# A state-space mixer with a top-1 mixture of experts: when the rows of the closing sum are fetched, and where the last expert units run

## The reference, cut to what matters

```
xn = layernorm(x)                                   # per token
proj = xn @ in_proj_w.T                             # gate 512 | x 512, B 128, C 128 | dt 64
xBC = silu(conv_b + causal 4-tap conv(xBC))
dt = softplus(dt + dt_bias);  A = -exp(A_log)       # 64 heads of 8
y = ssd(x * dt, dt * A, B, C) + D * x               # state recurrence along the sequence
hg = y * silu(gate)
s = (hg * rsqrt(mean(hg * hg) + 1e-5) * norm_w) @ out_proj_w.T

route = sigmoid(xn @ router_w)                      # 8 experts, each token goes to its best one
f = (silu(xn @ gate_w[e]) * (xn @ up_w[e])) @ down_w[e] * route[e]

out = x + s * silu(f)
```

## Time and profile before

| | |
|---|---|
| median of 3 runs | 488.84 us |
| the profiled execution | 490.0 us, its span 488.2 us |
| TensorE busy with matmuls | 417.5 us (86%), 2506 matmuls |
| TensorE loading weights | 340.5 us (70%) |
| VectorE | 310.7 us (64%), 675 instructions |
| ScalarE | 197.9 us (41%) |
| GpSimd | 215.8 us (44%) |
| moved by DMA | 81.43 MB, mean 167 GB/s |

### The profile page before, as it was taken

One profiled execution on the slowest core, in us unless ns is written; L12 is line 12 of the kernel. 1 busy time (PEld: TensorE's weight loads), 2 busy tenths in 40 slices (PEclk: granted clock), 3 DMA queues, 4 the chain that ended last, 5 costly groups with the idle time before them and its releaser, 6 DMA issues. The chain is left out here.

```text
span 488.2 us, 7643 instructions
## 1 busy us (share of the span) xinstructions
PE 417.5 (86%) x2506; PEld 340.5 (70%) x2506; DVE 310.7 (64%) x675; ACT 197.9 (41%) x490; POOL 215.8 (44%) x252
## 2 busy tenths in 40 slices
PE   0779376609999999999999999999989999998862
PEld 0775123409888797988788899788678878987752
DVE  4504975244598483769598664649687666667578
ACT  1552359310642626342633635442633662262100
POOL 3200471373018271718236455508236447776840
PEclk9999669757999999999999999999999999999785
DMA  8940126622464555776575563856575624313695
GB/s 274 287 118 1 49 104 230 203 83 88 142 178 167 178 182 180 186 225 186 186 209 194 155 211 118 222 187 173 178 213 186 159 99 127 108 57 100 193 349 188
DMA packets 56055, 81.43 MB, mean 167 GB/s; under 512 B 4720, under 2 KB 34416, under 8 KB 55888
## 3 DMA queue, kind: packets, MB, share of 16 engines
q1 hardware_dynamic: 54144, 75.81, 50.8%
q0 software_dynamic: 1872, 5.13, 2.9%
HBM read 64.37 MB, written 16.56 MB: 166 GB/s over the span
## 5 line engine op out<-in xcount | busy, mean ns | idle before, releaser
L577 POOL TENSOR_TENSOR ARENA<-ARENA 128x512 f32<-128x512 f32 (+1 forms) x80 | 105.1, 1323 | 7.8 <-ACT ARENA L782 2.8
L1009 PEld LDWEIGHTS BANK<-ARENA 128*128 128x128 f32 x736 | 87.6, 197 | 22.7 <-ACT ARENA L818 16.1
L1009 PE MATMUL BANK<-ARENA 128*128 128x128 f32 x736 | 89.1, 280 | 16.5 <-ACT ARENA L818 15.9
L629 POOL DMA_INDIRECT gate_rows<-ARENA x23 | 23.0, 998 | 155.8 <-DVE ARENA L1307 67.5
L899 PE MATMUL BANK<-ARENA,W_MAIN 128*128 128x512 f32 x160 | 80.5, 655 | 11.4 <-DVE ARENA L1206 11.4
L1187 DVE SCALAR_TENSOR_TENSOR ARENA<-BANK,CONVC,ARENA 128x511 f32<-128x511 f32 (+2 forms) x72 | 53.6, 748 | 28.1 <-ACT ARENA L725 15.9
L1042 DVE TENSOR_TENSOR ARENA<-ARENA,BANK 128x256 f32<-128x256 f32 (+1 forms) x128 | 57.5, 449 | 17.0 <-POOL ARENA L643 11.9
L899 PEld LDWEIGHTS BANK<-ARENA,W_MAIN 128*128 128x128 f32 x160 | 32.6, 213 | 49.4 <-issue 33.9
L1042 DVE TENSOR_TENSOR BANK<-BANK,ARENA 128x512 f32<-128x512 f32 (+1 forms) x80 | 50.6, 639 | 16.2 <-PE BANK L948 11.4
L957 PE MATMUL BANK<-ARENA 128*128 128x128 f32 x384 | 47.4, 280 | 2.8 <-POOL ARENA L577 2.2
L957 PEld LDWEIGHTS BANK<-ARENA 128*128 128x128 f32 x384 | 44.2, 192 | 4.1 <-issue 2.4
(11 more groups left out here) (130 smaller groups left out, 674.5 us busy)
## 6 DMA issues: line engine op xcount, KB each, us to landing
ARENA<-source_rows SPq DMA_DIRECT2D x96, 144.0 KB, 2.9
ARENA<-in_w_gate SPq DMA_DIRECT2D x23, 512.0 KB, 4.0
ARENA<-in_w_up SPq DMA_DIRECT2D x23, 512.0 KB, 4.9
ARENA<-in_w_down SPq DMA_DIRECT2D x23, 512.0 KB, 6.3
source_rows<-ARENA SPq DMA_DIRECT2D x16, 288.0 KB
ARENA<-in_x SPq DMA_DIRECT2D x8, 512.0 KB, 7.6
ARENA<-x_by_expert SPq DMA_DIRECT2D x23, 129.0 KB, 6.1
ARENA<-gate_rows SPq DMA_DIRECT2D x4, 512.0 KB, 8.2
```

Source lines behind the costliest of these rows:

```text
L577: nc.gpsimd.tensor_tensor(out=XS[par][rows, out_slot, 0:DIN].rearrange("p (a h) -> p a h", a=HD), in0=E2[par][rows, out_slot, :].unsqueeze ...
L629: pool.indirect_dma_start(out=g_dram, out_offset=bass.IndirectOffsetOnAxis(ap=TOKENS[:, t:t + 1], axis=0), in_=FY[par], in_offset=None).th ...
L1009: ins = nc.tensor.matmul(bank[:, f * P:(f + 1) * P], lhsT=WEXP[:, slot, at:at + P], rhs=FXT[par][:, j, :], start=(j == 0), stop=(j == DK - 1))
```

## The change

The new step `bring` (SyncE only) fetches what the closing sum needs beside the gate rows. `bring 0` to `2` are the tokens of groups 0 to 2, `bring 3` those of tiles 12 to 15, and `bring 4` to `6` the mixer rows of groups 0 to 2. The steps `load 0` to `3` now fetch gate rows alone. The buffers move: tokens go where the normalised inputs `XNT` were, and mixer rows and some gate rows go to the buffers of the convolution of even groups, which are free after tile 11. The two expert weight slots serve only gate rows. Expert units: tiles 0 to 10 take two, tiles 11 to 13 one, tiles 14 and 15 none. `fin 0` and `fin 1` stand ahead of `mid 15`, and `last 12` to `14` ahead of `tail 15`.

```diff
--- before.py
+++ after.py
@@ -114,17 +114,20 @@
 CHUNKS = {"rank": (1, 0), "conv": (0, 1), "flush": (0, 0), "pair": (3, 0), "head": (1, 1), "norm": (0, 0),
           "sort": (0, 0), "mid": (0, PAIRS + 3), "turn": (1, 0), "tail": (1, 0),
           "tx": (1, 0), "gu": (0, 2), "dn": (1, 0), "fy": (0, 0),
-          "rn": (0, 0), "load": (0, 0), "fin": (0, 0), "last": (0, 0)}
+          "rn": (0, 0), "bring": (0, 0), "load": (0, 0), "fin": (0, 0), "last": (0, 0)}
 ORDER = [*range(HB, BLOCKS), *range(HB)]
 SORT_AT = 2
 
 
-UNITS = [2] * 10 + [1] * 5
-TAIL_STEPS = {("tail", LAST - 1): [("rn", 0, 0)],
-              ("tail", LAST + 1): [("rn", 1, 0), *(("load", g, 0) for g in range(FIN + 1))],
-              ("mid", LAST + 3): [("fin", 0, 0), ("fin", 1, 0)],
-              ("tail", LAST + 2): [("rn", 2, 0)],
-              ("tail", LAST + 3): [("rn", 3, 0), ("fin", 2, 0), *(("last", LAST + c, 0) for c in range(GT))]}
+UNITS = [2] * 11 + [1] * 3
+TAIL_STEPS = {("tail", LAST - 1): [("rn", 0, 0), ("bring", 0, 0), ("bring", 1, 0)],
+              ("mid", LAST): [("bring", 2, 0), ("bring", 3, 0)],
+              ("tail", LAST): [("bring", 4, 0), ("bring", 5, 0)],
+              ("mid", LAST + 1): [("bring", 6, 0)],
+              ("head", LAST + 3): [("load", g, 0) for g in range(FIN + 1)],
+              ("tail", LAST + 1): [("rn", 1, 0), ("fin", 0, 0), ("fin", 1, 0)],
+              ("tail", LAST + 2): [("rn", 2, 0), ("fin", 2, 0), *(("last", LAST + c, 0) for c in range(FIN))],
+              ("tail", LAST + 3): [("rn", 3, 0), ("last", LAST + FIN, 0)]}
 RN_TILES = [(0, LAST), (LAST, LAST + 2), (LAST + 2, LAST + 3), (LAST + 3, LAST + 4)]
 
 
@@ -254,10 +257,12 @@
         CARRY = part(XB * (KC - 1)).rearrange("p (b j) -> p b j", b=XB)
         CTERM = part(XB * (KC - 1)).rearrange("p (b j) -> p b j", b=XB)
         XBC, GATE = [], []
+        conv_at = place[0]
         for _ in range(2):
             XBC.append(part(XB * GW).rearrange("p (b t) -> p b t", b=XB))
             GATE.append(part(HB * GW).rearrange("p (b t) -> p b t", b=HB))
         conv_end = place[0]
+        CONV0_FLAT = ARENA[:, conv_at:(conv_at + conv_end) // 2]
         WEXP = part(WSLOTS * WE).rearrange("p (e c) -> p e c", e=WSLOTS)
         FX = [part(XW) for _ in range(FXN)]
         FXT = [part(DM).rearrange("p (k t) -> p k t", k=DK) for _ in range(2)]
@@ -323,9 +328,9 @@
         def rows4(flat, n):
             return flat[:, n * GT * DM:(n + 1) * GT * DM].rearrange("p (t d) -> p t d", d=DM)
 
-        FIN_FLAT = [XNT_FLAT, WEXP[:, 0, :], WEXP[:, 1, :]]
-        ZG, ZX, ZO = ([rows4(flat, n) for flat in FIN_FLAT] for n in range(3))
-        LG, LX = rows4(BC_FLAT, 0), rows4(BC_FLAT, 1)
+        ZX, ZO = ([rows4(flat, n) for n in range(FIN)] for flat in (XNT_FLAT, CONV0_FLAT))
+        LX, LG = (rows4(flat, FIN) for flat in (XNT_FLAT, CONV0_FLAT))
+        ZG = [rows4(CONV0_FLAT, FIN + 1), rows4(WEXP[:, 0, :], 0), rows4(WEXP[:, 1, :], 0)]
 
 
         BANKS = [ctx.enter_context(nc.psum_tensor(f"BANK{i}", [P, 512], FP32)) for i in range(RING_A + RING_D)]
@@ -494,18 +499,24 @@
                     if t + FXN < NT:
                         sp.wait_ge(d_moved, d_of("gu", t, 1))
                         load_rows(t + FXN)
-                if kind == "load" and t < FIN:
-                    g, tiles = t, slice(t * GT, (t + 1) * GT)
+                if kind == "bring" and t <= FIN:
+                    if t == 0:
+                        sp.wait_ge(d_written, conv_of(GROUPS - 1, ORDER[-1]))
+                    rows = x_dram[:, t * GT:(t + 1) * GT, :]
+                    sp.dma_start(LX if t == FIN else ZX[t], rows).then_inc(fin_loaded[t], 16)
+                if kind == "bring" and t > FIN:
+                    g = t - FIN - 1
                     if g == 0:
+                        sp.wait_ge(hg_ready, LAST)
+                        for par in range(2):
+                            sp.wait_ge(o_stored[par], 16 * (LAST // 2))
+                    sp.dma_start(ZO[g], o_tiles[:, g * GT:(g + 1) * GT, :]).then_inc(fin_loaded[g], 16)
+                if kind == "load":
+                    if t == 0:
                         for par in range(2):
                             sp.wait_ge(g_scattered[par], 16 * ((NT + 1 - par) // 2))
-                            sp.wait_ge(o_stored[par], 16 * (LAST // 2))
-                    for to, rows in ((ZG[g], g_tiles), (ZX[g], x_dram), (ZO[g], o_tiles)):
-                        sp.dma_start(to, rows[:, tiles, :]).then_inc(fin_loaded[g], 16)
-                if kind == "load" and t == FIN:
-                    sp.wait_ge(d_written, d_of("head", TILES - 1))
-                    for to, rows in ((LG, g_tiles), (LX, x_dram)):
-                        sp.dma_start(to, rows[:, LAST:, :]).then_inc(fin_loaded[FIN], 16)
+                    rows = g_tiles[:, t * GT:(t + 1) * GT, :]
+                    sp.dma_start(LG if t == FIN else ZG[t], rows).then_inc(fin_loaded[t], 16)
                 if kind == "fin" and t > 0:
                     store_fin(t - 1)
                 if kind == "last":
```

## The result

The changed kernel takes 503.27 us (median of 4 runs, 502.52 to 504.41) against 488.79 us for the kernel before in the same runs. The ratio is 1.030, with a 95% interval from 1.028 to 1.033. The profiled execution took 503.3 us, its span is 501.5 us. The forecast was slower, 492.5 us, in a range of 488.6 to 495.8. The sign was right, and the size was a quarter of the measured one.

The account below looks back on a forecast made before the run. Bound: TensorE until 446.7 us, then a latency chain, SyncE to GpSimd to VectorE. Lost cover and queueing against 4.15 us saved put the last sum at 489.8, 3.8 us later; 488.84 + 3.7 gives 492.5 us, range 488.6 to 495.8.

Parts of the forecast that it names:

- Steps 1 to 3: Rows of tiles 13 and 14 through memory: first terms end at 445.2 (6.0 later) and 461.6 (against 455.4).
- the bounds: Limits on the last sum: lowest 486.8 with rounds of 10.0 to 10.2 us; highest adds 1.3, and 1 or 2.
- step 2: First term of tile 13 ends at 445.2; TensorE stalls about 4 us ahead of the new state's product.
- step 3: Tile 14: exponentials wait for GpSimd until 437.3 instead of 432.35; last pair there at 457.3, first term 461.6.
- rival C: TensorE's clock falls early, from 440 us; tile 15's write goes out some 3.5 us later; 495.0 us; chance 0.14.
- The step that failed: Tile 15's write at 453.4, behind 1.5 MB in SyncE's queue: 3.7 us to the reads at 457.1, last pair 469.3.
- Nothing waits for the data before 468 us: Closing-sum fetches: their only prices are contention in tiles 13 and 14 and their place ahead of tile 15's write.
- The early sums: Two group sums on VectorE between bodies 14 and 15: 5.6 us, 468.5 to 474.1; 1 or 2 more beside GpSimd.
- The end: Closing sum: last sum ends 7.8 us behind tile 15's body rather than 11.95, a saving of 4.15 us.
- Rival B: Loads behind the reads cost nothing, every round takes 10.0 to 10.2 us; 489.7 us; chance 0.16.
- Rival A: The cover suffices, tile 13's rows come in time: 1.8 us lost, 4.15 saved; 486.5 us, faster; chance 0.15.

Follow-up runs that it names:

- units_only: The kernel before with only the changed kernel's expert units (two in tile 10, one in tiles 11 to 13): 493.25 us against 488.41, ratio 1.009.
- mixer_late: The changed kernel with the three fetches of mixer rows moved behind the reads of tile 15: 496.6 us, ratio to before 1.017.
- units_mixer: The changed kernel with the expert units of before and mixer rows fetched behind tile 15's reads: 490.21 us, ratio to before 1.004.
- fin0_early: The kernel before, own units, with one group sum and its fetches moved ahead of the body of tile 15: 488.57 us, ratio 0.999.
- fin0_early_split: fin0_early with the last pair's two reads cut into six in every tile: 481.23 us, ratio to before 0.984.

## Why the prediction was wrong in size

| step | predicted us | measured us |
|---|---|---|
| 1 reads of tile 13 issued | 426.1 | 424.51 |
| 1 its last pair used | 437.0 | 437.42 |
| 2 first term of tile 13 ends | 445.2 | 445.16 |
| 3 write of tile 14 | 442.5 | 442.85 |
| 3 its last pair used | 457.3 | 457.51 |
| 3 first term of tile 14 ends | 461.6 | 461.63 |
| 4 body 14 ends | 468.5 | 468.5 |
| 4 `fin 0` starts | 468.5 | **476.59** |
| 4 both early sums done | 474.1 | 485.4 |
| 5 write of tile 15 | 453.4 | 452.60 |
| 5 reads of tile 15 issued | 457.1 | **462.31** |
| 5 its last pair used | 469.3 | 475.43 |
| 5 first term of tile 15 ends | 474.2 | 480.71 |
| 6 body 15 ends | 482.0 | 493.08 |
| 6 last sum ends | 489.8 | 499.34 |

**Steps 1 to 3 were right**, within 0.5 us but for the first reads. There two errors cancelled: the reads left 1.6 us sooner, and the round took 12.9 us instead of 10.9. `bring` behind the reads was thus dearer than I took it, above even the 12.2 of the bounds; without it, in units_only, the same round took 11.0 us (424.20 to 435.23). The gap of TensorE had another place than step 2 gave it. TensorE waited 3.1 us at head 14 for the exponentials of `pair 14`, which step 3 rightly had waiting for GpSimd, and the body then ran at the lower clock (24 matmuls in 4.64 us, where 2.87 is usual), so that the new state's product found its bank free:

```profile
438.43 1.12 PE L945 MATMUL BANK<-CONST,ARENA 128*128 128x128 f32 x4 [3.11 <-ACT ARENA L750]
...
441.37 4.64 PE L968 MATMUL BANK<-ARENA 128*128 128x128 f32 x24
```

The granted clock fell as rival C said, to 0.75 on average in 440 to 450 us, but ScalarE was released by VectorE for the head of tile 15 at 451.47, so the write was hardly later for it.

**The step that failed** is "The write stands in SyncE's queue close behind 1.5 MB ... I take 3.7". It took 9.7. The row I took it from had its weights issued 3 to 6 us before the write; here the fetches were issued 2 to 4 us before it, and these themselves lay behind reads that still had 8.5 us to run on a few engines. mixer_late shows the term by itself: 2.9 us without the fetches. A second term was left out. "Nothing waits for the data before 468 us" was true, but the gate rows' own landing I did not price at all. Issued at 466.47, behind the same kind of reads, they took 10.1 us, and `fin 0` started 8.1 us late. That is where 8.1 of the missing 9.5 us enter the chain. In mixer_late `fin 0` starts at 472.00, still 3.5 us behind 468.5, so some 4.6 of the 8.1 us are the write's and 3.5 the gate rows'; the order of the fetches is another there, which makes this a rough division.

**The early sums** were mis-sized: 8.8 us instead of 5.6, which adds 3.2. I had allowed 1 or 2. The same instruction takes 2.98 us beside GpSimd's work and 1.66 when GpSimd is all but idle (476.59 and 493.00 above), and the large addition 2.18 against 1.23. Traffic on the DMA engines is not the reason: before, the first one took 1.67 us at 474.00, with a DMA share of 0.87 in 470 to 480 us. By the Trainium skill (SBUF — State Buffer, "Who interferes with whom") an operation of VectorE with two inputs in SBUF contends with one of GpSimd that reads SBUF; the trace agrees, with GpSimd's 1.10 us operation stretched to 2.07 at 480.67. No kernel here took this contention away by itself.

**The end** was better than forecast: 6.3 us behind body 15 instead of 7.8. Projection 14 was still running when body 15 ended, so TensorE's clock had risen by projection 15 (its first eight matmuls in 1.97 us, where 3.75 were taken before), and VectorE's own 6.3 us of sums set the end.

8.1 + 3.2 - 1.5 is 9.8, against 9.5 us between forecast and trace; most of the rest is body 15, which was a little shorter.

**Two sums of the prediction do not follow.** Its own range, 490.8 to 494.5, is not what its bounds give: the lowest is 489.7, and the highest, with 1.3 and 1 or 2 us on 492.5, is 494.8 to 495.8. And in rival C the head ends at 455.7, which puts the write some 3.0 us later and not 3.5. Neither changes the answer.

**Rival B** fell on its own point: the rounds of tiles 13 and 14 took 12.9 and 12.5 us with loads behind the reads, against 11.0 and 10.0 in units_only. **Rival A** took the cover for sufficient, which units_only refutes, and the early sums for cheap: with the cover restored, units_mixer has nothing left of the 4.15 us.

## What to carry to other kernels

Before moving a fetch into a quiet stretch, look at what the latency chain writes and reads behind it on the same DMA engines, from any queue: a fetch of data that nobody waits for can hold up a small write that everything waits for. A read whose outermost dimension is 2 or 4 leaves a tail on few engines, which shows as 1 or 2 tenths of DMA share long after the issue; cutting it by rows was worth more here (6 us in the kernel before, and 17 us where fetches were queued behind it) than moving the fetches (none and 6.7 us). To find where such a gain comes from, count both traces from the same early event: here half of the 6 us came from the first tiles and not from the end. And work that is moved ahead of a step to fill TensorE takes cover away from the latency behind that step.

## What the runs showed of the hardware that was not expected

- Six DMAs instead of two for the same rows, with 2.75 us of issue instead of some 1.1, finish sooner: the tail at 2 and then 1 tenths of the DMA engines is gone.
- A second issuer (ScalarE) took the wait behind the write only from 9.7 to 7.8 us.
- Where no fetch lay between, the write of tile 15 landed 0.5 to 0.7 us after the last pair of the rows read ahead of it (before, units_only, mixer_late, fin0_early).
- VectorE's two-input operations on SBUF took up to 3.69 us for four of 128x256 beside GpSimd (fin0_early_split), where 1.66 is the time alone.
